# FFN weights in a stage of their own, four fusing blocks ahead of the first scores, and the first two rounds written out

## The chip, the cores and the metric
The kernel runs on one core of one Trainium2 chip. The metric is the device time of one execution in microseconds; times are compared by the median of several runs. A core has five engines that run side by side and meet at semaphores: TensorE (PE), VectorE (DVE), ScalarE (ACT), GpSimd (POOL), and SyncE (SP), which here issues all DMAs.

## The reference, cut to what matters
Eight batches of 128 tokens, width 512, in float32:

```
c  = x @ cond_weight[id]^T                 # condition, a weight for each batch
q, k, v = c @ Wq, c @ Wk, c @ Wv           # 32 query heads, 8 key groups, width 16
q, k = rope(q), rope(k)
ctx = softmax(causal(q k^T / 4)) v         # scores, maxima, exp, context
x1 = x + ctx @ Wo
h  = x1 @ W^T + 0.5 (x1 @ A[id]) @ B^T     # second condition, low rank
y  = x1 + h @ W_base^T + b + top-2 mixture of rank-16 experts of h
```

The last two lines are fused: the weights W and B are multiplied once with the FFN's weights (base, router, experts A, side by side 648 columns), so that each batch needs one projection of x1.

## The kernel before
Every float32 operand of a matmul is kept as a pair, a rounded high part (an ACT copy) and the low remainder (a subtraction on DVE or POOL), and a product is three matmuls: high by high, high by low, low by high. Weights come from memory into a stage and are split from there: Wq, Wk, Wv through `stage_a`, the second condition's W through `stage_b` (L281), W_o through `stage_b` again, the experts' B through `stage_c`, the first condition's weights through `cond_raw`. The FFN's weights (router, experts' A, base) also use `stage_a`, so SP waits for `qkv_lo` before it loads them (L284 to L289). `stage_a` later holds the exponentials for even keys, `probs_1` those for odd keys.

The ten blocks of `fuse(n)` (L1114) make the fused weight: n = 0 and 1 the low-rank rows (left and right 324 columns), n = 2 to 9 the four row tiles of W, left and right. Each block is 12 matmuls of 324 columns into one of two banks, `x_ps` and `c_ps` in turn; ACT copies its high part out and DVE its low part (`split_fused`), and a block waits until its bank is read (`fused_lo`). Each engine has an instruction order of its own, written by hand as a loop over rounds t = -1 to 6; in round t the batch f = t + 1 is conditioned and projected, batch t is scored, r = t - 1 goes through context and output, q = t - 2 through the experts. The fusing blocks stand in round t = 0, between the parts of batches 0 and 1. A batch's path on PE is `condition`, `transpose_c`, `project_q`, `project_kv`, `transpose_qk`, four `score` pieces, `transpose_maxima`, `score_t` twice and `context` twice. Between `project_kv` and `transpose_qk` DVE multiplies with the rope tables (`rotate_k`, `rotate_q`, L711 to L726) and POOL adds (`add_rotated`, L360). POOL's queue also holds the low parts of the condition weights (`split_condition`, L344) and of W_o (`split_output`, L349). DVE takes the row maxima of the scores (`maxima`, L647) and splits the experts' B (`split_experts`, L643) at the end of round 0, behind the last fusing block and ahead of `maxima(1, 0)`.

Every engine runs its queue in order: a wait holds all that is behind it.

Of the kernel before, what the change touches and what calls it, by code (L numbers as in the profile page):

```python
# [15 lines left out]
P = 128  # L16
# [3 lines left out]
def build_program(nc, x, x_t, cond_ids, lora_ids, cond_w_t, w_q, w_kv, w_o, cos, sin, w2, lora_a, lora_b,  # L20
# [34 lines left out]
    with ExitStack() as ctx:  # L55
# [55 lines left out]
        stage_b = sb("stage_b", [P, KT * D])  # L111
        stage_c = sb("stage_c", [P, D])
# [33 lines left out]
        probs_e = [stage_a, sb("probs_1", [P, KT * D])]  # L146
# [4 lines left out]
        ctx_n = sb("ctx_n", [P, D])  # L151
# [25 lines left out]
        o_in, w2_in, ffn_in, b_in, lb_in = sem("o_in"), sem("w2_in"), sem("ffn_in"), sem("b_in"), sem("lb_in")  # L177
# [44 lines left out]
        fused_ps = lambda n: (x_ps, c_ps)[n % 2][:, 0:HALF]  # L222
# [4 lines left out]
        ROUNDS = range(-1, BATCH - 1)  # L227
# [7 lines left out]
        def _(sp):  # L235
# [26 lines left out]

            def first_loads():
# [4 lines left out]
                stage_qkv = stage_a[:, :].rearrange("p (k n) -> p k n", k=KT)  # L268
                for k in range(KT):
                    sp.dma_start(stage_qkv[:, k, D:QKV], w_kv[k * P:(k + 1) * P, :]).then_inc(qkv_in[k], 16)  # L270
# [5 lines left out]
                for k in range(KT):  # L276
                    sp.dma_start(stage_qkv[:, k, 0:D], w_q[k * P:(k + 1) * P, :]).then_inc(qkv_in[k], 16)
                sp.dma_start(rope_cos[:, :], cos[0:P, :]).then_inc(tables_in, 16)
                sp.dma_start(rope_sin[:, :], sin[0:P, :]).then_inc(tables_in, 16)
                for k in range(KT):  # L280
                    sp.dma_start(stage_b[:, k * D:(k + 1) * D], w2[k * P:(k + 1) * P, :]).then_inc(w2_in, 16)  # L281
                sp.dma_start(lora_b_raw[:, :, :], lora_b.rearrange("(k p) r -> p k r", p=P)).then_inc(lb_in, 16)

            def later_weights():  # L284
                sp.wait_ge(qkv_lo, KT)
                stage_ffn = stage_a[:, 0:KT * FFN].rearrange("p (k n) -> p k n", k=KT)
                for src, at in ((router_t, 0), (experts_a_t, EXPERTS), (base_t, GATES)):
                    sp.dma_start(stage_ffn[:, :, at:at + src.shape[1]], src.rearrange("(k p) n -> p k n", p=P)
                                 ).then_inc(ffn_in, 16)  # L289
                sp.dma_start(bias_row[:, :], base_bias.partition_broadcast(P)).then_inc(bias_in, 16)  # L290
                sp.dma_start(stage_c[:, :], experts_b).then_inc(b_in, 16)
                sp.wait_ge(w2_lo, KT)
                sp.dma_start(stage_b[:, :].rearrange("p (k n) -> p k n", k=KT),
                             w_o.rearrange("(k p) n -> p k n", p=P)).then_inc(o_in, 16)

            first_loads()
            for t in ROUNDS:
# [3 lines left out]
                if t == -1:  # L301
                    later_weights()
# [11 lines left out]
        def _(pool):  # L314
# [39 lines left out]

            def split_a(b):
# [44 lines left out]
        def _(act):  # L400
# [15 lines left out]
            def split_qkv():  # L416
                for k in range(KT):
                    act.wait_ge(qkv_in[k], 32)
                    copy(qkv_w.hi[:, k, :], stage_a[:, k * QKV:(k + 1) * QKV]).then_inc(qkv_hi, 1)

            def split_second():
                act.wait_ge(w2_in, 16 * KT)
                for k in range(KT):
                    copy(w2_w.hi[:, k, :], stage_b[:, k * D:(k + 1) * D]).then_inc(w2_hi, 1)
# [3 lines left out]
            def split_ffn():  # L428
                act.wait_ge(ffn_in, 48)
                for k in range(KT):  # L430
                    copy(ffn_w.hi[:, k, :], stage_a[:, k * FFN:(k + 1) * FFN]).then_inc(ffn_hi, 1)
# [63 lines left out]
            def exp_scores(t, e):  # L495
                if t == 0 and e == 0:
                    act.wait_ge(ffn_lo, KT)
# [14 lines left out]
            split_xt(0)  # L512
            split_condition(0, range(KT))
            split_qkv()
            for t in ROUNDS:
# [8 lines left out]
                if t == 0:  # L524
                    split_fused(0)
                if batch(f):
                    split_c(f)
                if t == -1:
                    split_second()
# [3 lines left out]
                if t == 0:  # L533
                    split_fused(1)
                    split_fused(2)
                    split_fused(3)
# [6 lines left out]
                if t == -1:  # L543
                    split_ffn()
                if t == 0:
                    split_fused(4)
                if batch(t):
                    exp_scores(t, 0)
                if t == 0:
                    split_fused(5)  # L550
# [4 lines left out]
                if t == 0:  # L555
                    split_fused(6)
                    split_fused(7)
                if batch(t):
                    exp_scores(t, 1)
                if t == 0:  # L560
                    split_fused(8)
                    split_fused(9)
                    split_output()
# [22 lines left out]
        def _(dve):  # L586
# [21 lines left out]
            def split_first():  # L608
                for k in range(KT):
                    dve.wait_ge(cond_hi, k + 1)  # L610
                    low_of(cond_w.lo[:, k, :], cond_raw[:, k, :], cond_w.hi[:, k, :]).then_inc(cond_lo_first, 1)
                for k in range(KT):
                    dve.wait_ge(qkv_hi, k + 1)
                    low_of(qkv_w.lo[:, k, :], stage_a[:, k * QKV:(k + 1) * QKV], qkv_w.hi[:, k, :]
                           ).then_inc(qkv_lo, 1)
# [4 lines left out]
            def split_second():  # L620
                for k in range(KT):
                    dve.wait_ge(w2_hi, k + 1)
                    low_of(w2_w.lo[:, k, :], stage_b[:, k * D:(k + 1) * D], w2_w.hi[:, k, :]).then_inc(w2_lo, 1)
# [3 lines left out]
            def split_ffn():  # L627
                for k in range(KT):
                    dve.wait_ge(ffn_hi, k + 1)
                    low_of(ffn_w.lo[:, k, :], stage_a[:, k * FFN:(k + 1) * FFN], ffn_w.hi[:, k, :]  # L630
                           ).then_inc(ffn_lo, 1)
# [181 lines left out]
            split_first()  # L813
            for t in ROUNDS:
# [4 lines left out]
                if batch(t):  # L819
                    if t == 0:  # L820
                        dve.wait_ge(tables_made, 2)
# [5 lines left out]
                if t == 0:  # L827
                    split_fused(0)
# [6 lines left out]
                if t == 0:  # L835
                    split_fused(1)
                if batch(r):
                    scale_context(r, 0)
                if t == -1:
                    split_second()  # L840
# [13 lines left out]
                if t == 0:  # L854
                    split_fused(2)
                    split_fused(3)
# [5 lines left out]
                if t == 0:  # L862
                    split_fused(4)
                    split_fused(5)
# [8 lines left out]
                if t == -1:  # L873
                    split_ffn()
                if t == 0:
                    split_fused(6)
                    split_fused(7)
                    split_fused(8)
                    split_fused(9)
# [402 lines left out]
```

## Time and profile before

| | us |
|---|---|
| median of 3 runs (lowest, highest) | 268.69 (268.58, 269.58) |
| the profiled execution | 269.5 |
| its span, first to last instruction | 267.7 |
| PE busy | 237.8 (89%) |
| DVE busy | 182.6 (68%) |
| ACT busy | 117.9 (44%) |
| POOL busy | 86.7 (32%) |

Busy time says how long an engine had work under way; the wait of an engine is named in brackets behind an instruction in the timeline, with the operation that released it. Rounds of one batch take about 26.5 us in the middle of the kernel; the head before round 1 takes 65 us.

### The profile page before, as it was taken

To read this page: it belongs to the slowest core of one execution; us is meant where nothing else is said; L and a number is where in the kernel's file an instruction comes from. 1 tells how busy PE (TensorE), PEld (TensorE's weight loads), DVE (VectorE), ACT (ScalarE), POOL (GpSimd) and SP (SyncE) were. 2 spreads that over 40 slices of the span, in tenths; PEclk is the share of its full clock that TensorE was granted. 3 is DMA by queue.
4 is the path that set the end of the run, shared out by engine and by line. 5 is a ranking of instruction groups with operands and counts; after the bars stand their busy time and mean duration, and the time that the engine had idled before them with its cause. 6 is when DMAs were issued, how large, how long until landed. Compare 5 with 4: busy or idle time off the path is not lost.

```text
span 267.7 us, 5712 instructions
## 1 busy us (share of the span) xinstructions
PE 237.8 (89%) x2010; PEld 176.8 (66%) x2010; DVE 182.6 (68%) x908; ACT 117.9 (44%) x269; POOL 86.7 (32%) x92
## 2 busy tenths in 40 slices
PE   0565699999699999999999999999999999889994
PEld 0444588888376866586658765876587766556883
DVE  3583766441985689668965896589658966977653
ACT  2687233457607443643364336433642164054210
POOL 7207405322928005610562056205620050001010
PEclk9988689999989999999999999999999999999999
DMA  5999340041000700260027001600200030001111
GB/s 140 329 349 380 141 139 0 2 164 36 0 12 7 232 2 1 69 218 2 1 61 224 5 1 59 229 0 4 63 28 0 4 76 15 0 4 42 46 42 39
DMA packets 20000, 21.17 MB, mean 79 GB/s; under 512 B 6404, under 2 KB 11524, under 8 KB 19972
## 3 DMA queue, kind: packets, MB, share of 16 engines
q1 hardware_dynamic: 19972, 20.81, 24.5%
q8 instruction: 16, 0.26, 0.4%
q14 instruction: 12, 0.10, 0.1%
HBM read 18.71 MB, written 2.10 MB: 78 GB/s over the span
## 4 chain that ended last, share of the span: by engine, by line
PE 63%; DVE 20%; issue 7%; ACT 6%; SPq 1%; DMA 1%; POOL 0%; DVEq 0%
PE bank L932 9%; PE bank L927 9%; PE bank L928 8%; DVE thrown L655 7%; PE bank L1006 4%; PE bank L954 3%; PE bank L1020 3%; PE bank L1078 3%; PE bank L1021 3%; PE bank L1022 3%; PE bank L938 3%; PE bank L1133 2%; PE bank L981 2%; DVE turned L673 2%; PE bank L1134 2%
## 5 line engine op out<-in xcount | busy, mean ns | idle before, releaser
L346 POOL TENSOR_TENSOR cond_w_lo<-cond_raw,cond_w_hi 128x512 fp32r<-128x512 f32 x28 | 36.3, 1310 | 69.7 <-ACT cond_w_hi L402 69.7
L655 DVE CUSTOM_DVE_ANT_0 thrown<-bank,causal 128x128 f32<-128x128 f32 x256 | 56.0, 283 | 0.0
L362 POOL TENSOR_TENSOR rope_b<-rope_a,rope_b 128x128 f32<-128x128 f32 (+1 forms) x16 | 16.2, 1015 | 52.9 <-DVE rope_b L707 52.9
L927 PE MATMUL bank<-qkv_w_hi,c_t_hi 128*128 128x512 f32 (+1 forms) x64 | 22.5, 368 | 1.4 <-DVE c_t_lo L588 1.4
L1020 PE MATMUL bank<-cond_w_hi,xt_hi 128*128 128x512 f32 x32 | 14.7, 459 | 9.4 <-DVE cond_w_lo L588 9.4
L928 PE MATMUL bank<-qkv_w_lo,c_t_hi 128*128 128x512 f32 (+1 forms) x64 | 21.7, 355 | 0.0
L927 PE MATMUL bank<-fused_w_hi,late 128*128 128x324 f32 (+2 forms) x68 | 20.9, 322 | 0.0
L655 DVE DVE_READ_ACCUMULATOR2_ANT neg_max<- 128x1 f32 x256 | 20.6, 81 | 0.0
L371 POOL TENSOR_TENSOR x_bias<-x,bias_row 128x512 f32<-128x512 f32 x8 | 10.2, 1278 | 29.9 <-DVE out_sb L809 28.8
L928 PE MATMUL bank<-fused_w_lo,late 128*128 128x324 f32 (+2 forms) x68 | 19.9, 306 | 0.0
L402 ACT ACTIVATE cond_w_hi<-cond_raw 128x512 fp32r<-128x512 f32 x32 | 17.8, 622 | 4.0 <-DMA cond_raw<-cond_w_t 4.0
L502 ACT ACTIVATE probs<-bank 128x512 f32<-128x512 f32 x32 | 16.5, 604 | 6.6 <-PE bank L986 6.6
L402 ACT ACTIVATE turn<-bank 128x512 f32<-128x512 f32 x8 | 4.8, 598 | 31.6 <-PE bank L1022 31.5
L927 PEld LDWEIGHTS bank<-qkv_w_hi,c_t_hi 128*128 128x128 f32 x64 | 12.7, 199 | 9.0 <-issue 5.8
L502 ACT ACTIVATE stage_a<-bank 128x512 f32<-128x512 f32 x32 | 16.5, 603 | 1.1 <-PE bank L986 0.3
L402 ACT ACTIVATE v_ones<-bank 128x64 f32<-128x64 f32 x16 | 2.7, 221 | 32.0 <-PE bank L932 32.0
L402 ACT ACTIVATE late<-bank 128x128 fp32r<-128x128 f32 (+1 forms) x24 | 9.5, 397 | 16.3 <-PE bank L1100 10.6
L954 PE MATMUL bank<-k_pad_hi,q_t_hi 32*128 32x256 f32 x128 | 11.2, 339 | 5.3 <-DVE neg_max L655 3.2
L402 ACT ACTIVATE max_rows<-bank,own_p 128x128 fp32r<-128x128 f32 x32 | 9.1, 373 | 11.8 <-PE bank L964 11.8
L1020 PEld LDWEIGHTS bank<-cond_w_hi,xt_hi 128*128 128x128 f32 x32 | 6.9, 217 | 11.2 <-issue 9.6
L932 PE MATMUL bank<-qkv_w_hi,c_t_lo 128*128 128x512 f32 (+1 forms) x64 | 14.3, 346 | 0.0
L1021 PE MATMUL bank<-cond_w_lo,xt_hi 128*128 128x512 f32 x32 | 14.3, 446 | 0.0
(150 smaller groups left out, 629.8 us busy)
## 6 DMA issues: line engine op xcount, KB each, us to landing
cond_raw<-cond_w_t SPq DMA_DIRECT2D x7, 1024.0 KB, 5.5
xt_raw<-x_t SPq DMA_DIRECT2D x8, 256.0 KB, 5.9
x_nat<-x SPq DMA_DIRECT2D x8, 256.0 KB, 2.6
out<-out_sb SPq DMA_DIRECT2D x8, 256.0 KB, 2.0
cond_raw<-cond_w_t SPq DMA_DIRECT2D x4, 256.0 KB, 3.6
stage_a<-w_q SPq DMA_DIRECT2D x4, 256.0 KB, 5.3
stage_b<-w SPq DMA_DIRECT2D x4, 256.0 KB, 4.9
stage_a<-base_t SPq DMA_DIRECT2D x1, 1024.0 KB, 7.4
```

The costliest lines, as they stand in the source:

```text
L346: pool.tensor_tensor(cond_w.lo[:, k, :], cond_raw[:, k, :], f32(cond_w.hi[:, k, :]), ALU.subtract).then_inc(cond_lo, 1)
L362: pool.tensor_tensor(qk[:, at:at + w], rope_a[:, at:at + w], rope_b[:, at:at + w], ALU.add).then_inc(qk_ready, 1)
L402: return nc.scalar.activation(out, in_, ACT.Copy, scale=scale)
L502: nc.scalar.activation(probs_t[e][j], s_ps[j][:, :], ACT.Exp).then_inc(exped, 1)
L655: nc.vector.tensor_tensor_reduce(thrown[:, p % 2, j, e, :], s_ps[j][:, at:at + P], causal[:, :], -1.0, -MASKED, ALU.add, ALU.min, neg_max[ ...
L927: nc.tensor.matmul(out, lhs.hi[:, k, :], rhs.hi[:, k, cols], start=(k == 0), stop=False)
L928: nc.tensor.matmul(out, lhs.hi[:, k, :], rhs.lo[:, k, cols], start=False, stop=False)
L932: mm = nc.tensor.matmul(out, lhs.lo[:, k, :], rhs.hi[:, k, cols], start=False, stop=(last and k == KT - 1))
L954: mm = nc.tensor.matmul(s_ps[j][:, at:at + 2 * P], query[tile_rows(j), p, :], key[tile_rows(j), :, :], start=(n == 0), stop=(n == 2))
L1006: mm = nc.tensor.matmul(ctx_ps(r, e)[tile_rows(j), :], v_ones[r % 2][e][:, j, :, :], probs_t[e][j], start=True, stop=True)
L1020: nc.tensor.matmul(y_ps[:, :], xt.hi[:, k, :], cond_w.hi[:, k, :], start=(k == 0), stop=False)
L1021: nc.tensor.matmul(y_ps[:, :], xt.hi[:, k, :], cond_w.lo[:, k, :], start=False, stop=False)
```

## The change
Four things are changed. (1) The FFN's weights have a stage of their own, `stage_d`, which later holds the odd keys' exponentials and `ctx_n`; `probs_1` and the separate `ctx_n` are gone. They are loaded in `first_loads`: the low-rank B, router and experts' A ahead of the condition's weights, base in four parts behind the queries' and keys' weights, and W behind base. (2) Rounds -1 and 0 are written out, and the loop starts at t = 1. (3) On PE fuse(0), fuse(1) stand before `transpose_qk(0)`, fuse(2), fuse(3) before `score(0, 0)`, and the others one at a time further on; blocks 8 and 9 both use `x_ps`. (4) The experts' B is split on POOL, in round 1 behind `split_output`, no longer on DVE.

```diff
-        probs_e = [stage_a, sb("probs_1", [P, KT * D])]
+        probs_e = [stage_a, stage_d]
-        ctx_n = sb("ctx_n", [P, D])
+        ctx_n = stage_d[:, KT * D:KT * D + D]
-        fused_ps = lambda n: (x_ps, c_ps)[n % 2][:, 0:HALF]
+        fused_ps = lambda n: (c_ps if n % 2 and n < 8 else x_ps)[:, 0:HALF]
-        ROUNDS = range(-1, BATCH - 1)
+        ROUNDS = range(1, BATCH - 1)
 # SP, first_loads: ids, ids, xt, then
-                for k in range(KT):
-                    sp.dma_start(stage_qkv[:, k, D:QKV], w_kv[k * P:(k + 1) * P, :]).then_inc(qkv_in[k], 16)
+                sp.dma_start(lora_b_raw[:, :, :], lora_b.rearrange("(k p) r -> p k r", p=P)).then_inc(lb_in, 16)
+                for src, at in ((router_t, 0), (experts_a_t, EXPERTS)):
+                    sp.dma_start(stage_ffn[:, :, at:at + src.shape[1]], src.rearrange("(k p) n -> p k n", p=P)
+                                 ).then_inc(ffn_in, 16)
 # then the condition's four parts, w_kv and w_q by turns, cos, sin, and
+                for k in range(KT):
+                    sp.dma_start(stage_ffn[:, k, GATES:FFN], base_t[k * P:(k + 1) * P, :]).then_inc(base_in[k], 16)
+                for k in range(KT):
+                    sp.dma_start(stage_b[:, k * D:(k + 1) * D], w2[k * P:(k + 1) * P, :]).then_inc(w2_in[k], 16)
             first_loads()
+            load_condition(1)
+            later_weights()
+            load_condition(2)
+            load_batch(0)
 # POOL
+            def split_experts():
+                pool.wait_ge(b_hi, 1)
+                pool.tensor_tensor(moe_b.lo, stage_c[:, :], f32(moe_b.hi), ALU.subtract).then_inc(b_lo, 1)
+            for f in range(2):
+                split_condition(f + 1, 0)
+                split_condition(f + 1, 1)
+                add_rotated(f, rope_k, D, KV)
+                add_rotated(f, rope_q, 0, D)
+                split_condition(f + 1, 2)
+                split_condition(f + 1, 3)
+                split_xt(f + 1)
                 if t == 1:
                     split_output()
+                    split_experts()
 # ACT, in order: split_xt(0), split_rank(), split_condition(0, range(KT)), then
+            split_qkv(0)
+            split_qkv(1)
+            split_qkv(2)
+            copy_c(0)
+            split_qkv(3)
+            split_c(0)
+            for k in range(KT):
+                split_ffn(k)
+            copy_v(0)
+            for k in range(KT):
+                split_second(k)
+            split_fused(0)
+            split_condition(1, range(2))
+            split_fused(1)
+            split_qk(0)
+            split_fused(2)
+            split_condition(1, range(2, KT))
+            split_xt(1)
+            split_fused(3)
+            split_fused(4)
+            copy_c(1)
+            split_fused(5)
+            split_c(1)
+            split_fused(6)
+            split_condition(2, range(KT))
+            split_xt(2)
+            split_fused(7)
+            copy_v(1)
+            spread_maxima(0)
+            exp_scores(0, 0)
+            split_qk(1)
+            split_fused(8)
+            exp_scores(0, 1)
+            split_fused(9)
+            split_a(0)
+            split_output()
 # DVE, after owns, the splits of condition 0, rank, qkv, c(0) and sign_sin
+            for k in range(KT):
+                split_ffn(k)
+            split_second(0)
+            rotate_k(0)
+            rotate_q(0)
+            split_second(1)
+            split_second(2)
+            split_second(3)
+            split_fused(0)
+            split_fused(1)
+            split_k(0)
+            split_q(0)
+            split_fused(2)
+            split_fused(3)
+            split_fused(4)
+            dve.wait_ge(tables_made, 2)
+            maxima(0, 0)
+            maxima(0, 1)
+            split_fused(5)
+            split_c(1)
+            split_fused(6)
+            maxima(0, 2)
+            maxima(0, 3)
+            split_maxima(0)
+            split_fused(7)
+            rotate_k(1)
+            rotate_q(1)
+            split_k(1)
+            split_q(1)
+            split_fused(8)
+            split_fused(9)
-            def split_experts():
-                dve.wait_ge(b_hi, 1)
-                low_of(moe_b.lo, stage_c[:, :], moe_b.hi).then_inc(b_lo, 1)
 # PE
-                    pe.wait_ge(fused_lo, n - 1)
-                if n == 5:
-                    pe.wait_ge(max_spread, 1)
+                    pe.wait_ge(fused_lo, n - 1 if n < FUSED - 1 else n)
+            condition(0)
+            transpose_c(0)
+            project_q(0)
+            project_kv(0)
+            fuse(0)
+            fuse(1)
+            transpose_qk(0)
+            fuse(2)
+            fuse(3)
+            score(0, 0)
+            score(0, 1)
+            fuse(4)
+            condition(1)
+            fuse(5)
+            transpose_c(1)
+            score(0, 2)
+            score(0, 3)
+            fuse(6)
+            project_q(1)
+            fuse(7)
+            project_kv(1)
+            transpose_maxima(0)
+            score_t(0, 0)
+            fuse(8)
+            transpose_qk(1)
+            score_t(0, 1)
+            fuse(9)
+            score(1, 0)
+            score(1, 1)
```

## Rows read from the trace of the kernel before

**Rows 1.** The page: busy us by engine, and the chain by engine.
```profile
PE 237.8 (89%) x2010; PEld 176.8 (66%) x2010; DVE 182.6 (68%) x908; ACT 117.9 (44%) x269; POOL 86.7 (32%) x92
...
PE 63%; DVE 20%; issue 7%; ACT 6%; SPq 1%; DMA 1%; POOL 0%; DVEq 0%
```

**Rows 2.** Stage table: length, busy us by engine, PE clock, DMA share, GB/s.
```profile
30.00:60.00 30.00, 29.89 (x250) 26.22 (x254) 17.82 (x92) 11.64 (x28) 8.04 (x7) 0.91 0.27 90
...
95.00:121.50 26.50, 25.77 (x231) 18.45 (x231) 20.21 (x109) 12.58 (x30) 10.22 (x9) 1.00 0.23 73
```

**Rows 3.** PE timeline: start, us, operation, count, idle before and its releaser.
```profile
23.03 0.64 PE L932 MATMUL bank<-qkv_w_hi,c_t_lo 128*128 128x256 f32 x4
27.29 0.33 PE L1047 MATMUL bank<-ident,rope_b 128*128 128x128 f32 x1 [3.62 <-POOL rope_b L362]
...
30.11 0.59 PE L954 MATMUL bank<-k_pad_hi,q_t_hi 32*128 32x256 f32 x4 [2.05 <-DVE q_t_lo L737]
...
36.37 0.31 PE L1134 MATMUL bank<-shared,lora_bw_hi 128*128 128x324 f32 x1
...
64.99 0.50 PE L1020 MATMUL bank<-cond_w_hi,xt_hi 128*128 128x512 f32 x1
...
67.97 1.07 PE L1006 MATMUL bank<-stage_a,v_ones 128*32 128x512 f32 x8
...
71.78 0.39 PE L954 MATMUL bank<-k_pad_hi,q_t_hi 32*128 32x256 f32 x4 [2.15 <-DVE neg_max L655]
...
72.69 1.82 PE L1006 MATMUL bank<-probs,v_ones 128*32 128x512 f32 x8
...
79.58 0.27 PE L964 MATMUL bank<-ident,max_cols 128*128 128x128 f32 x1
```

**Rows 4.** Stage table, two stretches of 1 us with the granted clock.
```profile
34.00:35.00 1.00, 1.00 (x4) 0.81 (x3) 1.00 (x12) 0.00 (x0) 0.00 (x0) 0.50 1.07 330
...
74.00:75.00 1.00, 1.00 (x5) 0.50 (x2) 1.00 (x11) 0.00 (x0) 1.00 (x1) 0.50 0.00 0
```

**Rows 5.** ACT timeline.
```profile
16.90 2.19 ACT L402 ACTIVATE late<-stage_b 128x512 fp32r<-128x512 f32 x4
...
23.70 0.34 ACT L402 ACTIVATE v_ones<-bank 128x64 f32<-128x64 f32 x2 [1.14 <-PE bank L932]
...
38.20 0.44 ACT L402 ACTIVATE lora_g<-bank 128x324 fp32r<-128x324 f32 x1 [1.18 <-PE bank L1135]
...
64.52 2.18 ACT L402 ACTIVATE shared<-stage_b 128x512 fp32r<-128x512 f32 x4
```

**Rows 6.** DVE timeline; the two L655 rows are maxima in a row.
```profile
17.56 2.50 DVE L588 TENSOR_TENSOR late<-stage_b,late 128x512 fp32r<-128x512 f32 x4
...
67.26 1.07 DVE L588 TENSOR_TENSOR shared<-stage_c,shared 128x512 fp32r<-128x512 f32 x1 [2.10 <-ACT shared L402]
68.26 0.28 DVE L655 CUSTOM_DVE_ANT_0 thrown<-bank,causal 128x128 f32<-128x128 f32 x1
...
68.47 0.28 DVE L655 CUSTOM_DVE_ANT_0 thrown<-bank,causal 128x128 f32<-128x128 f32 x1
```

**Rows 7.** POOL timeline.
```profile
20.56 3.78 POOL L346 TENSOR_TENSOR cond_w_lo<-cond_raw,cond_w_hi 128x512 fp32r<-128x512 f32 x3 [12.44 <-ACT cond_w_hi L402]
24.71 0.46 POOL L362 TENSOR_TENSOR rope_b<-rope_a,rope_b 128x128 f32<-128x128 f32 x1 [0.37 <-DVE rope_b L707]
25.97 1.27 POOL L362 TENSOR_TENSOR rope_b<-rope_a,rope_b 128x512 f32<-128x512 f32 x1 [0.80 <-DVE rope_b L707]
...
82.05 1.68 POOL L362 TENSOR_TENSOR rope_b<-rope_a,rope_b 128x512 f32<-128x512 f32 x1 [0.80 <-DVE rope_b L707]
```

**Rows 8.** SP's issues in the timeline, and the page's DMA issues.
```profile
1.91 1.92 SPq L270 DMA_DIRECT2D stage_a<-w_kv  x4
...
12.98 0.39 SPq L243 DMA_DIRECT2D cond_raw<-cond_w_t  x1
...
cond_raw<-cond_w_t SPq DMA_DIRECT2D x7, 1024.0 KB, 5.5
```

More of the change, by code:

```diff
@@ L111, in build_program @@
         stage_b = sb("stage_b", [P, KT * D])
+        stage_d = sb("stage_d", [P, KT * FFN])
         stage_c = sb("stage_c", [P, D])
@@ L176, in build_program @@
         cond_first_in = [sem(f"cond_first_in{k}") for k in range(KT)]
-        o_in, w2_in, ffn_in, b_in, lb_in = sem("o_in"), sem("w2_in"), sem("ffn_in"), sem("b_in"), sem("lb_in")
+        w2_in = [sem(f"w2_in{k}") for k in range(KT)]
+        base_in = [sem(f"base_in{k}") for k in range(KT)]
+        o_in, ffn_in, b_in, lb_in = sem("o_in"), sem("ffn_in"), sem("b_in"), sem("lb_in")
         out_free = sem("out_free")
@@ L414, in split_condition, with split_qkv, split_rank, split_second @@
                     copy(cond_w.hi[:, k, :], cond_raw[:, k, :]).then_inc(cond_hi, 1)
[L416 to L424, printed above, removed]
+            def split_qkv(k):
+                act.wait_ge(qkv_in[k], 32)
+                copy(qkv_w.hi[:, k, :], stage_a[:, k * QKV:(k + 1) * QKV]).then_inc(qkv_hi, 1)
+            def split_rank():
                 act.wait_ge(lb_in, 16)
                 copy(lora_bw.hi[:, :, :, :], four_times(lora_b_raw)).then_inc(lb_hi, 1)
[L428 to L431, printed above, removed]
+            def split_second(k):
+                act.wait_ge(w2_in[k], 16)
+                copy(w2_w.hi[:, k, :], stage_b[:, k * D:(k + 1) * D]).then_inc(w2_hi, 1)
+            def split_ffn(k):
+                act.wait_ge(ffn_in, 32)
+                act.wait_ge(base_in[k], 16)
+                copy(ffn_w.hi[:, k, :], stage_d[:, k * FFN:(k + 1) * FFN]).then_inc(ffn_hi, 1)
             def split_fused(n):
@@ L495, in exp_scores @@
             def exp_scores(t, e):
[L496 to L497 removed]
+                if t == 0:
+                    act.wait_ge((qkv_lo, ffn_lo)[e], KT)
                 if t > 0:
@@ L606, in owns, with split_condition, split_qkv, sign_sin @@
                 nc.vector.tensor_copy(later_b[:, :, :], later[:, :, :]).then_inc(owns_made, 1)
[L608 to L615, printed above, removed]
+            def split_condition(k):
+                dve.wait_ge(cond_hi, k + 1)
+                low_of(cond_w.lo[:, k, :], cond_raw[:, k, :], cond_w.hi[:, k, :]).then_inc(cond_lo_first, 1)
+            def split_qkv(k):
+                dve.wait_ge(qkv_hi, k + 1)
+                low_of(qkv_w.lo[:, k, :], stage_a[:, k * QKV:(k + 1) * QKV], qkv_w.hi[:, k, :]).then_inc(qkv_lo, 1)
+            def sign_sin():
                 dve.wait_ge(tables_in, 32)
@@ L618, in split_first, with split_rank, split_second, split_ffn @@
                                         ).then_inc(sin_signed, 1)
[L620 to L623, printed above, removed]
+            def split_rank():
                 dve.wait_ge(lb_hi, 1)
                 low_of(lora_bw.lo[:, :, :, :], four_times(lora_b_raw), lora_bw.hi[:, :, :, :]).then_inc(lb_lo, 1)
[L627 to L631, printed above, removed]
+            def split_second(k):
+                dve.wait_ge(w2_hi, k + 1)
+                low_of(w2_w.lo[:, k, :], stage_b[:, k * D:(k + 1) * D], w2_w.hi[:, k, :]).then_inc(w2_lo, 1)
+            def split_ffn(k):
+                dve.wait_ge(ffn_hi, k + 1)
+                low_of(ffn_w.lo[:, k, :], stage_d[:, k * FFN:(k + 1) * FFN], ffn_w.hi[:, k, :]).then_inc(ffn_lo, 1)
             def split_fused(n):
@@ L812, in _ @@
             owns()
-            split_first()
+            for k in range(KT):
+                split_condition(k)
+            split_rank()
+            for k in range(KT):
+                split_qkv(k)
+            split_c(0)
+            sign_sin()
+            for k in range(KT):
+                split_ffn(k)
[28 more added lines that the diff above has]
+            split_fused(9)
             for t in ROUNDS:
@@ L872, in _ @@
                     split_q(f)
[L873 to L879, printed above, removed]
-                    split_experts()
                 if batch(r):
@@ L1159, in _ @@
                     transpose_c(f)
-                if t == 0:
-                    fuse(1)
                 if batch(t):
@@ L1164, in _ @@
                     score(t, 3)
-                if t == 0:
-                    fuse(2)
                 if batch(q):
@@ L1181, in _ @@
                     score_t(t, 0)
-                if t == 0:
-                    fuse(5)
                 if batch(r):
@@ L1200, in _ @@
                     project_ffn(r, 0, left_ps(r)).then_inc(gates_done, 1)
-                if t >= 0 and batch(f):
+                if batch(f):
                     score(f, 0)
```

67 lines of the change are left out of this document (5 added, 62 removed).

## The prediction

> **What bounds the kernel now.** The page's busy line is read first, then the chain [rows 1]: TensorE (PE) is busy for 89% of the span and holds 63% of the chain, VectorE (DVE) 20%. Two stretches of the stage table show how far that goes [rows 2]: from 30 to 60 us PE is busy for 29.89 of 30, and in a steady round (95 to 121.5) for 25.77 of 26.5. So the steady rounds have nothing to give. The diff touches only the head (start to 65 us, where the stage weights are split, batches 0 and 1 begin and the ten blocks of `fuse` run) and round t = 1 behind it. The PE timeline shows what PE loses there [rows 3]: 3.62 us before `transpose_qk(0)` at 27.29 (waiting for POOL's rotated queries), 2.05 us before `score(0,0)` at 30.11, and, in round 1, 2.15 us before `score(1,2)` at 71.78. After the gaps the granted clock is 0.50, the 1.2 GHz level [rows 4]: at 34 us, and again at 74 us. The slow stretch is a cost of its own: the eight context matmuls at 72.69 took 1.82 us, the same at 67.97 took 1.07.
>
> **Loads and the first projections.** Instead of four w_kv issues (1.92 us from 1.91) [rows 8], SP issues three small ones ahead of the condition weights; that can bring condition(0) forward by at most some 0.6 us. ACT's fourth qkv copy now stands between copy_c(0) and split_c(0), which gives it back. I take project_q(0) as unmoved, so project_kv(0) ends near 23.6 [rows 3], with 0.5 us either way for the range. The FFN's weights no longer wait for stage_a: their splitting on ACT and DVE (about 3 us each) falls into the 17 to 21 us stretch beside the projections; nothing is charged.
>
> **fuse(0) and fuse(1) into the first gap.** One matmul of a block follows the other by 0.15 us (0.31 is the pipelined length) [rows 3], so a block of 12 costs 1.77 us at 2.4 GHz. Two of them fill 23.6 to 27.1, all but 0.1 us of the 3.62 gap. But the rotated sum comes later. ACT now does copy_v(0) first (to 24.0), then the four copies of w2 (2.19), split_fused(0) (0.44) [rows 5], and only then the two first copies of condition 1, 0.55 each: the first lies at 26.7 + 0.55 = 27.2. POOL's queue is strict: two condition splits (a third of 3.78, 1.26 each), the key sum 0.46 and the query sum 1.27 [rows 7] follow, 4.25 us, so 31.45. Before, three such splits were done by 24.34. DVE's rotation also waits for split_second(0), a copy and a split (1.2 us) later than before, which is hidden under POOL's queue.
>
> To this a collision is added. DVE's split_second(1..3) (2.50 / 4 = 0.63 each [rows 6]) read two SBUF tiles and now run beside these POOL sums. Where such a DVE instruction stood beside a POOL one before, the query sum took 1.68 [rows 7] against the 1.27 of the first, +0.4, and DVE's expert split took 1.07 us [rows 6] where w2's took 0.63. Three meetings add 0 to 1.4 us; I take three, as the orders start at the same moment: the transposes start at 32.8, against 27.29. The Trainium skill, "SBUF — State Buffer", section "SBUF: two separate sides", says that a DVE operation with two SBUF inputs and a GpSimd operation exclude each other for the whole instruction; by that three whole DVE splits, 3 x 0.63 = 1.9 us, would stand in POOL's way and the transposes would start at 33.3. The row's +0.4 is part of a DVE instruction that had already begun, so it agrees.
>
> **fuse(2) and fuse(3) into the second gap.** PE was idle from 27.1 to 32.8, so it comes back at the slow level: before, the work that followed the idle ran at 1.2 GHz until 35.3, that is for 5 us [rows 3, 4]. I charge one block at half clock, 3.3 us; the ends are no block (1.8) and two (6.6 for both). Transposes 0.65 (estimated, 0.45 at full clock), fuse(2) 3.3, fuse(3) 1.77, the two scores 0.91 at full clock (72.69 less 71.78), fuse(4) 1.77: 41.2. condition(1) needs POOL's two last splits and xt, whose ACT copies are queued behind split_fused(2): 36.8 + 0.44 + 0.55, then 3 x 1.26 gives 41.6. So condition(1) starts at 41.6 against some 31.7 before (behind the scores of 30.11), with five blocks (8.85 us) done instead of none. It then takes 2.8 us at full clock, where it took 4.5, to the first block, whose second matmul is at 36.37.
>
> **The rest of the head.** From 44.4 PE has fuse(5) 1.77, transposes 0.45, scores 0.91, fuse(6) 1.77, project_q 2.8 (12 matmuls of 512 columns like condition(2) from 64.99, 0.235 each), fuse(7) 1.77, project_kv 1.42: 55.35. DVE's maxima(0,0..1) are now queued behind split_fused(4): 42.3 + 3.4 (16 maxima, 0.21 apart [rows 6]) = 45.7, before the 46.65 at which PE asks. maxima(0,2..3), behind split_fused(6), end at 54, before 55.35. Then transpose of maxima 0.3, ACT's spreading 1.3, to 57.4; fuse(8) to 59.2, transpose_qk(1) to 59.8, score_t(0,1) to 61.3. fuse(8) and fuse(9) share one bank, and fuse(9) waits for split_fused(8), which ACT and DVE do behind the queries and keys of batch 1: 62.2, a new wait of 0.9. With fuse(9) and two scores condition(2) starts at 64.9, against 64.99. The head gains 0.1 us: 8 us of gaps and slow clock were there, and POOL's queue, one slow block and the fuse(9) wait take nearly all of it back.
>
> **Round 1.** Before, DVE took up maxima(1,0) only after split_experts, at 68.3: it had waited 2.10 us for ACT's copy (behind split_output, 2.18 from 64.52), then 1.07 of its own [rows 5, 6]. Now POOL does that split, where its first user is finish_ffn(0) in round 2. DVE goes from split_fused(9), done at 65.0, straight into maxima(1,0..1), ready at 68.4. PE needs condition 2.8, context 0.98 and transposes 0.5 from 64.9, so score(1,2) starts at 69.25, not 71.78: 2.4 us. With no idle before it the clock stays at 2.4 GHz: 0.8 us from the context and some 0.9 from the first project_q matmuls, of which four ran at 0.43 in place of 0.235 [rows 4]. Then DVE is the later one: split_c, scaling, maxima(1,2), turn, maxima(1,3) end at 75.7 where PE is ready at 75.4, -0.3. transpose_maxima(1) starts at 75.7, before 79.58 [rows 3]: 3.9 us. split_experts adds 1.3 us to POOL: split_output and it end near 71.9, the next condition splits and split_a at 76.4, the rotated queries are due at about 77.9. Hidden, by 0.7 us with the key sum; if that cover goes, it costs what is over. The rounds behind are unchanged and PE bound, so the gain stays.
>
> **Sum.** 0.1 + 3.8 = 3.9 us. The profiled execution took 269.5 us (span 267.7); 265.6 would come of it. The median of the runs is 0.8 lower, 268.69, and the forecast against it is 264.8. Own range: the collision (0 to 1.4, 1.9 by the lock), the slow blocks (-1.5 to +1.8), the start (0.5 either way): 262.5 to 267.
>
> **Rivals.** (A) The blocks fill both gaps whole, POOL's sums not delayed. Then the head gains the 3.62 + 2.05 and some 2.5 of slow clock, 8.2, and with round 1 the time is 256.6. For it: the gaps are that wide. Against: POOL's order puts two splits ahead, and their ACT copies lie behind w2's. A milder form, in which the clock is full from the transposes on, gives 263. (B) Only the head's shift counts: the POOL sums in round 1 or DVE become the bound and take the 3.9 us back, same time as before, 268.6. For: DVE is busy 20 of 26.5 us in a round and its slack at split_maxima is negative by 0.3. Against: DVE's wait before 67.26 is plain, and the maxima beside POOL's splits there are only 0.21 apart [rows 6]. (C) Slower: the second condition lands late. It is now issued behind base and w2, at about 15.5 instead of 12.98 [rows 8]. POOL's sums wait for its splits, so from 26.7 each microsecond of lateness is one of the time; by 3.9 us, at 30.6, the gain is gone, and at 33 the time is 271. For: it now stands at the end of a queue of more than 4 MB. Against: a 1 MB load took 5.5 us [rows 8], which gives 21.5, and with 2 us more for the queue 23.5, 3 us ahead of need. (D) The slow clock holds two blocks and the collisions are whole: 264.8 + 1.8 + 0.5 = 267.1, with little more slower still.
>
> **Chances.** Forecast with its own range 0.72, A and its milder form 0.10, B 0.07, C 0.05, D and beyond 0.06. The range for 8 in 10: 262.2 to 267.4. What a measurement here can tell from no change is about 0.5%, 1.3 us: faster 0.82, same 0.11, slower 0.07.
>
> **What would show it.** After: PE's first transposes of qk near 32.8 with POOL as releaser; fuse(2) in part at 1.2 GHz; a wait of PE before fuse(9) for DVE's fused_w_lo; condition(2) within 1.5 us of 65; DVE's maxima(1,0) right behind split_fused(9); no granted 0.50 at 70 to 80; transpose_maxima(1) near 75.7 and all behind it equally early. Wrong: transposes near 28, condition(1)'s weights landing behind 27, POOL's rotated queries releasing PE in round 1, or a steady round longer than 26.5.

## The result and the profile after

The changed kernel took 267.95 us (median of 20 runs, 266.65 to 269.06), the kernel before beside it 269.49 us (20 runs, 267.65 to 271.27): ratio 0.995, 95% interval 0.9932 to 0.9967. A second comparison (experiment 5) gave 267.9 against 269.12, ratio 0.996 (0.9935 to 0.9985). The change is worth about 1.3 us (the medians of this comparison differ by 1.5) where 3.9 were forecast, and the forecast of 264.8 us (262.2 to 267.4) was missed.

The page of the changed kernel, busy time and chain, against [rows 1]:

```profile
span 266.2 us, 5719 instructions
...
PE 236.3 (89%) x2010; PEld 176.9 (66%) x2010; DVE 184.0 (69%) x907; ACT 117.8 (44%) x269; POOL 88.7 (33%) x93
...
PE 62%; DVE 18%; ACT 7%; issue 7%; POOL 2%; DMA 1%; SPq 1%; DVEq 0%; ACTq 0%
```

Hardly anything moves in the totals. The PE timeline shows the places [rows 3] (start, us, operation, count, idle before and its releaser):

```profile
32.50 0.48 PE L1092 MATMUL bank<-ident,rope_b 128*128 128x128 f32 x1 [5.33 <-POOL rope_b L372]
32.77 1.06 PE L983 MATMUL bank<-ident,rope_b 128*128 128x128 f32 x4
...
39.30 0.39 PE L999 MATMUL bank<-k_pad_hi,q_t_hi 32*128 32x256 f32 x4
...
42.09 0.40 PE L1065 MATMUL bank<-cond_w_hi,xt_hi 128*128 128x512 f32 x1
...
62.95 0.41 PE L1176 MATMUL bank<-shared,late 128*128 128x324 f32 x1 [0.85 <-DVE fused_w_lo L622]
...
65.81 0.51 PE L1065 MATMUL bank<-cond_w_hi,xt_hi 128*128 128x512 f32 x1
...
70.37 0.39 PE L999 MATMUL bank<-k_pad_hi,q_t_hi 32*128 32x256 f32 x4
...
71.29 1.07 PE L1051 MATMUL bank<-stage_d,v_ones 128*32 128x512 f32 x8
...
77.63 0.33 PE L1009 MATMUL bank<-ident,max_cols 128*128 128x128 f32 x1 [0.56 <-DVE max_cols L695]
```

The gap before the first transposes is one of 5.33 us at 32.50, with POOL as releaser; the second gap, at the first score, is gone; condition(2), the end of the head, starts at 65.81, 0.8 us later than before (64.99); score(1,2) has no wait any more; transpose_maxima(1) starts at 77.63, 1.95 us earlier than 79.58. In the later rounds 0.4 us of that is lost, in steps in rounds 3 (0.1) and 5 (0.3); the cause stays open. The span ends 1.5 us earlier.

The stage table (length, busy us by engine, granted clock, DMA share, GB/s), against [rows 4]:

```profile
34.00:37.00 3.00, 3.00 (x13) 3.00 (x12) 1.20 (x3) 0.98 (x3) 0.00 (x0) 0.50 0.45 171
37.00:38.00 1.00, 1.00 (x6) 1.00 (x5) 0.42 (x1) 0.89 (x3) 0.00 (x0) 0.50 0.00 0
38.00:66.00 28.00, 27.06 (x264) 23.01 (x264) 14.34 (x90) 15.04 (x36) 11.79 (x10) 1.00 0.21 69
66.00:94.00 28.00, 26.78 (x233) 19.45 (x233) 21.47 (x127) 14.78 (x34) 16.51 (x14) 1.00 0.30 99
```

After the long gap TensorE works at 1.2 GHz up to 38 us; from there on, round 1 included, at 2.4 GHz. POOL's and DVE's timelines, against [rows 6, 7]:

```profile
27.01 3.35 POOL L352 TENSOR_TENSOR cond_w_lo<-cond_raw,cond_w_hi 128x512 fp32r<-128x512 f32 x2 [18.88 <-ACT cond_w_hi L421]
30.32 2.12 POOL L372 TENSOR_TENSOR rope_b<-rope_a,rope_b 128x128 f32<-128x128 f32 x2
...
71.46 1.28 POOL L363 TENSOR_TENSOR shared<-stage_c,shared 128x512 fp32r<-128x512 f32 x1
```

```profile
26.89 4.02 DVE L622 TENSOR_TENSOR late<-stage_b,late 128x512 fp32r<-128x512 f32 x3
...
65.94 0.29 DVE L685 CUSTOM_DVE_ANT_0 thrown<-bank,causal 128x128 f32<-128x128 f32 x1
...
71.99 1.03 DVE L712 TENSOR_TENSOR scaled<-turned,inv_sum 128x256 f32<-128x256 f32 x1
...
77.77 0.42 DVE L712 TENSOR_TENSOR scaled<-turned,inv_sum 128x256 f32<-128x256 f32 x1
```

Three splits of W took DVE 4.02 us beside POOL's splits and sums, where four took 2.50 alone; maxima(1,0) starts at 65.94, straight behind split_fused(9), as forecast.

### The profile page after: what moved, and what is told of

Read it like the earlier page. It is cut to its first block, busy times and chain, and to the rows that moved or that the text cites. A ratio compares the mean times of both kernels' runs of the same rounds, so it can differ in the third digit from the quotient of the medians.

```text
span 266.2 us, 5719 instructions
## 1 busy us (share of the span) xinstructions
PE 236.3 (89%) x2010; PEld 176.9 (66%) x2010; DVE 184.0 (69%) x907; ACT 117.8 (44%) x269; POOL 88.7 (33%) x93
## 4 chain that ended last, share of the span: by engine, by line
PE 62%; DVE 18%; ACT 7%; issue 7%; POOL 2%; DMA 1%; SPq 1%; DVEq 0%; ACTq 0%
PE bank L972 9%; PE bank L977 8%; PE bank L973 8%; DVE thrown L685 7%; PE bank L1051 3%; PE bank L1065 3%; PE bank L1123 3%; PE bank L999 3%; PE bank L1066 3%; PE bank L1067 3%; PE bank L983 3%; DVE turned L703 2%; PE bank L1176 2%; ACT late L421 2%; PE bank L1026 2%
## 5 line engine op out<-in xcount | busy, mean ns | idle before, releaser
L352 POOL TENSOR_TENSOR cond_w_lo<-cond_raw,cond_w_hi 128x512 fp32r<-128x512 f32 x28 | 37.4, 1350 | 80.2 <-ACT cond_w_hi L421 80.2
L1065 PE MATMUL bank<-cond_w_hi,xt_hi 128*128 128x512 f32 x32 | 13.8, 431 | 9.4 <-DVE cond_w_lo L622 9.4
L521 ACT ACTIVATE stage_d<-bank 128x512 f32<-128x512 f32 x32 | 16.5, 603 | 5.6 <-PE bank L1031 5.5
L972 PE MATMUL bank<-shared,late 128*128 128x512 f32 x32 | 13.1, 409 | 1.1 <-issue 0.7
L622 DVE TENSOR_TENSOR late<-bank,late 128x512 fp32r<-128x512 f32 (+1 forms) x16 | 7.8, 489 | 9.0 <-ACT late L421 9.0
L973 PEld LDWEIGHTS bank<-qkv_w_lo,c_t_hi 128*128 128x128 f32 x64 | 12.6, 197 | 1.5
```

The costliest lines, as they stand in the source:

```text
L352: pool.tensor_tensor(cond_w.lo[:, k, :], cond_raw[:, k, :], f32(cond_w.hi[:, k, :]), ALU.subtract).then_inc(cond_lo, 1)
L521: nc.scalar.activation(probs_t[e][j], s_ps[j][:, :], ACT.Exp).then_inc(exped, 1)
L972: nc.tensor.matmul(out, lhs.hi[:, k, :], rhs.hi[:, k, cols], start=(k == 0), stop=False)
L973: nc.tensor.matmul(out, lhs.hi[:, k, :], rhs.lo[:, k, cols], start=False, stop=False)
L1065: nc.tensor.matmul(y_ps[:, :], xt.hi[:, k, :], cond_w.hi[:, k, :], start=(k == 0), stop=False)
```

## The experiments

Every experiment was timed against the kernel before in the same rounds. The changed kernel stood beside the fifth to eighth only. Differences from the changed kernel are given as differences of the medians. The ratios to the kernel before give the same within 0.4 us, but for the third and fourth experiments (six executions each), where they give about 3 us instead of the 2.2 and 2.1 below.

**1. The experts' split alone.** The kernel before, with one edit:

```diff
                 if t == 1:
                     split_output()
+                    split_experts()      # POOL; DVE's at the end of round 0 is gone
```

> The kernel before with one part of the change alone: the experts' low part is made on POOL in round 1, behind the output weights' splits, instead of on DVE at the end of round 0. Theory H (the head of the changed kernel is worth nothing or costs up to 1 us, round 1 alone gives the gain): score(1,2) starts 2 to 2.5 us earlier than 71.8, no 1.2 GHz stretch follows, 2.5 to 3.5 us faster than before, and so 1 to 2 us faster than the changed kernel. Rival R (the gain of round 1 needs the earlier state that the new head leaves): within 1 us of before. Rival S (POOL takes it back, its rotated queries come late): POOL releases transpose_qk(2), gain under 1 us.

266.69 us against 269.28, ratio 0.9906 (0.9871 to 0.994): 2.6 us, twice what the whole change gives. In its PE timeline there is no wait at score(1,2) (71.43), and in DVE's none before the maxima:

```profile
28.52 0.47 PE L1047 MATMUL bank<-ident,rope_b 128*128 128x128 f32 x1 [3.62 <-POOL rope_b L366]
...
31.89 0.59 PE L954 MATMUL bank<-k_pad_hi,q_t_hi 32*128 32x256 f32 x4 [2.05 <-DVE q_t_lo L738]
...
71.43 0.39 PE L954 MATMUL bank<-k_pad_hi,q_t_hi 32*128 32x256 f32 x4
...
78.26 0.33 PE L964 MATMUL bank<-ident,max_cols 128*128 128x128 f32 x1 [0.46 <-DVE max_cols L666]
```

The old head's two gaps stand as they were. The profiled execution was one of the slow ones of its twelve (268.74 us, mean granted clock 0.966), so the places of its head say little; from condition(2), at 66.86, to transpose_maxima(1) it took 11.4 us where before it was 14.6. Theory H came out, and rivals R and S did not (nothing on POOL releases transpose_qk(2)): the gain is round 1's. By this comparison the rest of the change (stage, loads, order of the blocks) costs some 1.2 us, the difference of the ratios; their intervals, from different comparisons, overlap a little (0.9932 to 0.994), and the second experiment gives another value.

**2. The experts' split back on DVE** in the changed kernel (behind split_fused(9)).

> The changed kernel with the experts' low part back on DVE behind split_fused(9). In the changed kernel ACT's copy of it ended at 68.5, so DVE would take up maxima(1,0) near 69.5 instead of 65.9. Theory H: 2.5 to 3.5 us slower than the changed kernel, so 1 to 2 us slower than before, with PE's wait at score(1,2) and a 1.2 GHz stretch after it back. Rival R (the head gives part of the gain, round 1 the rest): as fast as before or up to 1 us faster.

268.61 us against 269.28, ratio 0.9962 (0.9926 to 0.9998): only some 0.7 us slower than the changed kernel, not 2.5 to 3.5, and 0.7 us faster than before, not slower. That is rival R's number. The profiled execution alone does show what theory H expected, a span of 268.9 us and

```profile
73.12 0.39 PE L999 MATMUL bank<-k_pad_hi,q_t_hi 32*128 32x256 f32 x4 [2.56 <-DVE neg_max L684]
```

with a stretch of 1.2 GHz behind it (mean granted clock 0.974). But 7 of the 12 executions had a mean granted clock of 0.985 or 0.986 and took 267.8 to 268.8. The likeliest reading is that the gap is not followed by the slow stretch in every execution, and that the 1.7 us which the forecast booked for it are had in some only; where in an unprofiled execution the clock was low isn't recorded, so this is inferred, not shown. The parts of the change do not add up, then: the new head costs some 1.2 us when the experts' split is on POOL (first experiment) and gives some 0.7 us when it is on DVE (this one). No run explains the difference. How far one kernel's time moves with the clock shows in the kernel before: at a mean granted clock of 0.973 or 0.974 its executions beside the first four experiments took 268.8 to 270.1, at 0.978 or 0.979 268.0 to 268.4, at 0.961 to 0.968 270.9 to 271.6.

**3. POOL's rotated sums first.**

```diff
+                add_rotated(0, rope_k, D, KV)      # for f = 0 ahead of both splits
+                add_rotated(0, rope_q, 0, D)
                 split_condition(1, 0)
                 split_condition(1, 1)
```

> The changed kernel with POOL's sums of the rotated keys and queries of batch 0 ahead of the two splits of condition 1. The sums then follow DVE's rotation, which ended at 26.9, so transpose_qk(0) starts near 28.5 instead of 32.5, with some 1.3 us of idle before it. Theory P (POOL's queue order is what the head pays): scores 4 us earlier, less what then limits: fuse(2) waits for the split of W on DVE (done near 29) and condition(1) for its low parts, whose copies ACT makes behind split_fused(2); 2 to 4 us faster than the changed kernel, no 1.2 GHz stretch behind 28, or a short one. Rival Q (the head is held by PE's own work or by ACT, and the order on POOL only moves idle time): under 1 us faster.

265.71 us against 269.28, ratio 0.9832 (0.9781 to 0.9882): 2.2 us faster than the changed kernel. In the profile the transposes start 3 us earlier (29.45, forecast near 28.5) and condition(1) 1.4 us earlier:

```profile
29.45 0.33 PE L1096 MATMUL bank<-ident,rope_b 128*128 128x128 f32 x1 [1.58 <-POOL rope_b L372]
...
32.28 0.61 PE L1180 MATMUL bank<-shared,late 128*128 128x324 f32 x1 [2.07 <-DVE lora_g L626]
...
40.70 0.47 PE L1069 MATMUL bank<-cond_w_hi,xt_hi 128*128 128x512 f32 x1 [0.31 <-issue]
```

The rest turns into a wait of fuse(2) for split_fused(0), which on DVE stands behind the three splits of W; these collide with POOL's condition splits as in the changed kernel (4.02 us again). A slow stretch remains behind this wait, from 32 to some 35.5 us, and it is shorter than the changed kernel's. Theory P has the size, 2 to 4 us, but how much of it is POOL's order and how much the shorter slow stretch isn't told apart here.

**4. The clock kept up in the gap.**

```diff
             fuse(1)
+            pe.wait_ge(owns_made, 7)
+            for _ in range(30):
+                nc.tensor.matmul(s_ps[0][:, 0:D - P], ident_b[:, :], later_b[:, 0:PAIRS - 1, :], start=True, stop=True)
             transpose_qk(0)
```

> The changed kernel with 30 matmuls without a use (384 columns, bfloat16, into a score bank that is not yet in use) between fuse(1) and transpose_qk(0), about 4.8 us in the 5.3 us in which PE is idle. Theory C (the 1.2 GHz stretch after the gap costs what it holds: 7 of 12 matmuls and more of fuse(2) and the transposes, 32.5 to 37.6): the granted clock stays 1.00 from 24 us on, fuse(2) takes 1.8 instead of 3.4, 1.5 to 2.2 us faster than the changed kernel. Rival D (condition(1)'s low parts, made on POOL behind ACT's copies, set the pace there, so the clock costs nothing): under 0.5 us faster.

265.85 us against 269.28, ratio 0.9842 (0.9792 to 0.9893): 2.1 us faster, without one useful instruction more.

```profile
32.43 0.33 PE L1092 MATMUL bank<-ident,rope_b 128*128 128x128 f32 x1 [0.45 <-POOL rope_b L372]
...
39.93 0.47 PE L1065 MATMUL bank<-cond_w_hi,xt_hi 128*128 128x512 f32 x1 [0.32 <-issue]
```

The transposes start where they did, and condition(1) starts 2.16 us earlier than in the changed kernel's profile (42.09). That is the price of the slow stretch in the head in this pair of profiles, and the medians say the same; rival D falls.

**5. The changed kernel again.**

> The changed kernel itself, beside the others of this call. All theories: 0.995 of before, 268 us or a little under.

267.9 us against 269.12, as told above. Its profiled execution had a mean granted clock of 0.974 and a span of 267.4 us, 1.2 us over the first profile, and all of it in the head: condition(2) starts at 67.27 instead of 65.81. The head is the same up to the first scores in the second, fifth and sixth experiments, gap included, and the slow stretch behind the gap is not. Transposes and first scores in these three profiles, in this order:

```profile
33.28 0.47 PE L1092 MATMUL bank<-ident,rope_b 128*128 128x128 f32 x1 [5.33 <-POOL rope_b L368]
38.88 0.39 PE L999 MATMUL bank<-k_pad_hi,q_t_hi 32*128 32x256 f32 x4
...
33.70 0.47 PE L1092 MATMUL bank<-ident,rope_b 128*128 128x128 f32 x1 [5.34 <-POOL rope_b L372]
40.74 0.39 PE L999 MATMUL bank<-k_pad_hi,q_t_hi 32*128 32x256 f32 x4
...
32.43 0.48 PE L1092 MATMUL bank<-ident,rope_b 128*128 128x128 f32 x1 [5.33 <-POOL rope_b L372]
38.14 0.39 PE L999 MATMUL bank<-k_pad_hi,q_t_hi 32*128 32x256 f32 x4
```

From the transposes to the scores 5.60, 7.04 and 5.71 us go by, and 6.80 in the changed kernel's first profile. The granted clock is back at 1.00 at about 36, 40 and 36 us, and at 38 in the first profile.

**6. Block 8's split first.**

```diff
-            split_qk(1)            # ACT; on DVE the same with split_k(1), split_q(1)
             split_fused(8)
+            split_qk(1)
```

> The changed kernel with split_fused(8) ahead of split_qk(1) on ACT and ahead of split_k(1) and split_q(1) on DVE. Theory W (fuse(9)'s wait of 0.86 us for its bank is on the path): the wait goes, condition(2) and all behind it start 0.8 us earlier, 0.6 to 0.9 us faster than the changed kernel. Rival V (what waits next, exp_scores(0,1) or the low parts of condition 2 on POOL, keeps the end of the head where it is): under 0.2 us.

267.06 us against 269.12, ratio 0.9927 (0.9897 to 0.9958): 0.8 us under the changed kernel beside it, the size of theory W. The wait before fuse(9) is gone; a smaller one comes in its place, at score(1,0) for ACT's exponentials:

```profile
63.71 0.39 PE L999 MATMUL bank<-k_pad_hi,q_t_hi 32*128 32x256 f32 x4 [0.33 <-ACT stage_d L521]
```

The intervals of the two overlap. The trace gives a size that is free of the head's clock, since it can be counted from condition(1): 23.24 us to condition(2) instead of 23.72, and 11.44 us from there to transpose_maxima(1) instead of 11.82. That is 0.5 us from the wait and 0.4 us from round 1, where DVE's scaling of the context met POOL's experts' split nearer its end (it took 1.03 us in the changed kernel):

```profile
70.80 0.66 DVE L712 TENSOR_TENSOR scaled<-turned,inv_sum 128x256 f32<-128x256 f32 x1
```

So theory W has the sum, but only half of it by its own mechanism; rival V, under 0.2 us, falls.

**7. The splits of W ahead of the rotations.**

```diff
             split_second(0)
-            rotate_k(0)
-            rotate_q(0)
             split_second(1)
             split_second(2)
             split_second(3)
+            rotate_k(0)
+            rotate_q(0)
```

> The changed kernel with all four DVE splits of W ahead of the rotations of batch 0, so that none of them runs beside POOL's sums. ACT's last copy of W ends at 26.1, so DVE's rotations run from 26.8 to 28.8, still ahead of POOL's adds. Theory L (DVE instructions with two SBUF operands hold POOL up: its splits of condition 1 took 3.35 for two where 2.52 is usual, the query sum with the key sum 2.12 where 1.73): transpose_qk(0) starts 1.1 to 1.3 us earlier than 32.5, the time is 0.5 to 1.2 us lower. Rival M (POOL is held by ACT's copies or memory): transpose_qk(0) stays within 0.3 us of 32.5.

265.9 us against 269.12, ratio 0.9884 (0.9851 to 0.9918): 2.0 us. No split of W runs beside a POOL sum now, and both are at their own pace:

```profile
27.04 2.49 POOL L352 TENSOR_TENSOR cond_w_lo<-cond_raw,cond_w_hi 128x512 fp32r<-128x512 f32 x2 [18.89 <-ACT cond_w_hi L421]
29.49 1.68 POOL L372 TENSOR_TENSOR rope_b<-rope_a,rope_b 128x128 f32<-128x128 f32 x2
```

```profile
24.59 2.50 DVE L622 TENSOR_TENSOR late<-stage_b,late 128x512 fp32r<-128x512 f32 x4 [3.96 <-ACT late L421]
```

transpose_qk(0) starts at 31.22, 1.28 us earlier: theory L, with its size. The time falls by more than expected. In this profile the slow stretch is shorter too (mean granted clock 0.987, against 0.981 in the changed kernel's): from the transposes to condition(1) it is 8.96 us instead of 9.59. So part of the 2.0 is the clock's; how much was not measured apart.

**8. The three edits together** (3, 6, and 9 and 12 matmuls without a use in the gaps that 3 leaves).

> The changed kernel with three edits: POOL's rotated sums of batch 0 ahead of its condition splits, split_fused(8) ahead of batch 1's queries and keys, and 9 and 12 matmuls without a use in the two gaps that are left (ahead of transpose_qk(0) and of fuse(2)). Alone these were worth 2.3 us (order), 0.8 expected, and the clock 2.1. If they add: head 1.3 (order) + 1.3 (clock from the gaps left) + 0.8, 263 to 264.5 us. Rival (after the order is right the slow clock and the order are the same microseconds): 264.5 to 265.5.

263.36 us against 269.12, ratio 0.9789 (0.9756 to 0.9823), 4.5 us under the changed kernel. The expectation's own terms sum to 3.4 us and the three edits measured alone to 5.1 (2.2, 0.8 and 2.1); the measured 4.5 lies between. The rival's 264.5 to 265.5 is missed by over 1 us: the order and the clock are not the same microseconds.

**9. The old head, filled.** The first experiment, with 20 such matmuls ahead of transpose_qk(0) and 11 ahead of score(0,0).

> The kernel before with the experts' low part on POOL (as the first experiment) and matmuls without a use in the two gaps of the old head: 20 (384 columns, bfloat16, into a score bank not yet in use) ahead of transpose_qk(0), 11 ahead of score(0,0). Nothing of the new head. Theory K (half of what the old head lost is the slow clock, which needs no new order): the granted clock stays 1.00 from 22 us, scores and condition(1) take 3.7 instead of 6.1 us, 264 to 264.7 us. Rival (what follows condition(1) in the old head waits for something else, as for the maxima on DVE): over 265.5 us.

264.67 us against 269.34, ratio 0.9828 (0.9784 to 0.9872): 2.0 us under the first experiment, theory K's number. The old order of the blocks, with the clock kept up, is 3.2 us faster than the changed kernel:

```profile
27.72 0.33 PE L1047 MATMUL bank<-ident,rope_b 128*128 128x128 f32 x1 [0.36 <-POOL rope_b L366]
...
30.54 0.39 PE L954 MATMUL bank<-k_pad_hi,q_t_hi 32*128 32x256 f32 x4 [0.26 <-DVE q_t_lo L738]
```

Beside the fourth experiment this compares the two heads with the clock kept up in both: the old one ends (condition(2)) at 63.08, the new one at 63.74. So the new order is 0.7 us behind even where its slow stretch is gone; the medians, 264.67 and 265.85, differ by 1.2 and the ratios by 0.4.

**10. The first gaps too**: the eighth, with 3 and 8 more ahead of transpose_c(0) and project_q(0).

> The kernel of the eighth experiment with 3 and 8 more matmuls without a use in the waits of PE around transpose_c(0), so that the 1.2 GHz stretch at 17 to 21 us, in project_q(0), goes too. Theory C: project_q(0) takes 2.8 instead of some 4.3 us, 1.0 to 1.6 us faster than that kernel, 261.8 to 262.4 us. Rival: project_q(0) shortens, but the copies of W on ACT behind copy_v(0), which now start earlier, are then held by DMA or by the FFN's splits: under 0.5 us.

262.27 us against 269.34, ratio 0.9744 (0.9701 to 0.9787), 1.1 us under the eighth. All of project_q(0) runs at 2.4 GHz:

```profile
18.00:24.00 6.00, 6.00 (x38) 5.45 (x38) 3.58 (x7) 2.98 (x7) 0.00 (x0) 1.00 1.05 371
```

It is the fastest version, 5.6 us under the changed kernel.

## Why the prediction was wrong

Counted against the profiled execution the forecast was 265.6 us; that of the changed kernel took 267.95, 2.35 us more. Three terms make it up: 0.9 us in the head, 1.0 in round 1, 0.4 in the later rounds. A fourth lies in the yardstick.

*The slow clock behind the gap in the head, the first step that failed, by its size.* The forecast charged one block at half clock. In the trace the transposes (32.50 to 33.5), all of fuse(2) and the start of fuse(3) ran at 1.2 GHz, until 37.95: from the transposes to score(0,0) 6.80 us went by, not 5.7. The prediction had read a slow stretch of 5 us off the rows of before and charged 4 of them (transposes and one block, 0.65 + 3.3); 5.5 were measured. In part it is luck which value one gets: behind the same gap two of the four profiles (experiments 2 and 6) show the 5.7 as charged, two the 6.8 and 7.0, so what failed is a fixed charge for something that varies by 1.4 us. At full clock this stretch took 4.23 us (fourth experiment, 32.43 to 36.66), so the slow clock lengthened it by 2.6 us where 1.7 had been charged; 2.1 of the 2.6 arrive at condition(1) and in the medians. The gap that causes it is one that the change itself made, 5.33 us in one piece instead of 3.62 and 2.05.

The rest of the head came nearly as worked out: transposes at 32.50 (forecast 32.8), fuse(9)'s new wait 0.85 us (0.9), and the loads hidden. Of the 1.1 us too much, 0.5 arrived at condition(1), at 42.09 for 41.6, as PE had been forecast to wait there for POOL's splits anyway. Another 0.4 us came between condition(1) and condition(2), 23.7 us for 23.3, in small pieces which no run tells apart. (Where the prediction goes from 55.35 to 57.4, its two terms give only 1.6 us; 2.07 were measured, from 55.92 to 57.99.) So the head ended at 65.8 and not at 64.9, and turned from +0.1 into a loss of 0.8 us. The forecast's own range had two slow blocks in it, but not together with the next term.

*Round 1, the second, and the firmer of the two.* The forecast had 10.8 us from condition(2) to transpose_maxima(1); it took 11.8 (before 14.6), in this profile and in those of the third, fourth, fifth and seventh experiments alike (11.80 to 11.82). So the term of 3.8 us was 2.8. The chain is DVE's, as forecast. One collision was not charged: the scaling of the context (71.99) took 1.03 us, where before it took 0.54 at this place and takes 0.42 undisturbed (77.77), as it met the experts' split that the change had itself put on POOL (71.46 to 72.74). In the first, sixth, eighth, ninth and tenth experiments the scaling meets that split nearer its end and takes 0.60 to 0.66, and the same stretch takes 11.40 to 11.44 us. So this meeting cost 0.4 of the 1.0. Another 0.2 was lost before score(1,2) (4.56 us from condition(2), forecast 4.35). The remaining 0.4 is not assigned, as the prediction doesn't give DVE's pieces one by one; in the trace DVE waits 0.52 us for PE's context and 0.47 for ACT's copy of c. And the second experiment suggests that the part of the term that is clock is had in some executions only. That the experts' wait was nevertheless what pays in this change, the first experiment confirms.

*Later rounds.* "The rounds behind are unchanged and PE bound, so the gain stays" was nearly right: 0.4 us were lost there. Most of it lies between transpose_maxima(4) and transpose_maxima(5): 26.84 us before and 26.81 in the second experiment, the two kernels with the experts' split on DVE, and 27.16 to 27.22 in all ten others, with the split on POOL. So the loss goes with the moved split; by what way is open.

*The yardstick.* The median shown of before, 268.69, was of three runs. Over 20 runs it was 269.49, and the profiled execution of 269.5 was the typical one, not one 0.8 too slow. This put another 0.8 us into the forecast time, none into the gain.

*What was right.* POOL's queue is what holds the first transposes: in the third experiment they start 3 us earlier. The collision, three meetings, was charged with 1.35 us; the seventh experiment gives 1.28. By the lock of the Trainium skill ("SBUF — State Buffer", "SBUF: two separate sides") three whole DVE splits would have stood in POOL's way, by estimate 1.9 us. Two of POOL's splits and its two adds took 5.47 us beside DVE and 4.17 alone, 1.3 more, so the measurement lies under that; that POOL was not last at every meeting would explain it and isn't shown. DVE itself lost more: 4.02 us for three splits, where four took 2.50 alone. That is the exclusion, seen from the other side.

*The rivals.* A and C did not happen: the gaps were not filled, and ACT's copies of the second condition did not wait for their load. B, same time as before, was near in size (1.3 us against its 0). Its mechanism had a small part: POOL's rotated queries released nothing, but DVE's collision took 0.4 us back, and the head gave away the rest. D, two slow blocks and whole collisions, 267.1 us, comes nearest to what the profile shows of the clock, some 5.5 us of slow work; the collisions stayed at 1.3 us.

## What to carry to other kernels

When a change moves work around an idle gap of TensorE, ask what becomes of the gap's length and put the clock after it into the sum in full, with a range: here 5.3 us of idle cost another 2.1 us in slow matmuls behind it, and thirty matmuls without a use bought these back. Before moving useful work into a gap, look at the in-order queue of the engine that releases it: two sums placed ahead of two splits gave 2.2 us, more than the whole change, part of it by a shorter slow stretch. And judge a change made of several edits edit by edit, since one that pays (2.6 us) can hide that the others cost; then try them together as well, since here the parts did not add up.

## What the runs showed of the hardware

- One and the same gap of 5.33 us was followed by slow work of different length: from the transposes to the scores 5.60, 5.71, 6.80 and 7.04 us in four profiles. One profile is one draw of this.
- Executions of one kernel differ in their mean granted clock, which took a few values (0.961, 0.968, 0.973, 0.979 for the kernel before), and there the time went with it, 271.6 to 268.0 us. With the gaps filled (tenth experiment, 0.997 to 1.0) the six executions lie within 1.2 us (261.88 to 263.07). What is left there is not the clock: the three at 1.0 were the slower ones.
- A DVE instruction with two operands in SBUF waits for a POOL instruction under way and the other way round: 1.34 us for each split of W instead of 0.63, POOL's condition splits 1.68 instead of 1.25 (changed kernel and seventh experiment). The row maxima, with one operand in PSUM, stay 0.21 us apart beside POOL's work (66.5 to 69.3).
- Where two such instructions meet depends on a few tenths of a microsecond: the scaling of the context in round 1 took 1.02 or 1.03 us in five profiles and 0.60 to 0.66 in five others, and the round went with it, 11.8 and 11.4 us.
